# A mixture-of-experts and attention block on one core: PSUM ring banks in the true order of products, the router's products moved beside the projections, three groups of routed rows, another order of the last batch

## The reference, cut to what matters

```python
x = L0_attn_x
xn = _layernorm(x, axis=-1)
x = x + _L0_attn_ref(xn, ...) + _L0_ffn_ref(xn, ...)
# in _L0_ffn_ref:
scores = jnp.einsum("bqhd,bkhd->bhqk", q, k) * scale
probs = jax.nn.softmax(scores, axis=-1)
attn = jnp.einsum("bhqk,bkhd->bqhd", probs, v).reshape(B, T, D_MODEL)
x = _layer_norm(src + attn @ Wo + bo, ln1_g, ln1_b)
keys = (x @ router_w + router_b)[..., 0]
expert_idx = jnp.remainder(jnp.floor(keys).astype(jnp.int32), N_EXPERTS)
h = jax.nn.relu(x @ W1[e] + b1[e]); y = h @ W2[e] + b2[e]   # e = expert_idx
return _layer_norm(x + ff_out, ln2_g, ln2_b)
```

## Time and profile before

| | |
|---|---|
| median of 3 runs | 2028.31 us (2026.37 to 2028.73) |
| the profiled execution | 2027.01 us, span 2025.2 us, so 1.8 us lie around the span |
| plain attention with its end, routing | span start to 723 us |
| experts | 723 to 968 us |
| rotary attention | 968 us to the end |
| busy over the span: PE, DVE, POOL, ACT | 1809.4, 1314.8, 983.4, 829.1 us |

### The profile page before, as it was taken

How to read it: one execution, slowest core, us unless ns; L and a number is a source line. 1 busy time by engine, 2 the same in 40 slices (tenths; PEclk the granted TensorE clock), 3 DMA queues, 4 the chain that set the end, 5 groups by cost and what they waited for, 6 DMA issues and landing times.

```text
span 2025.2 us, 32126 instructions
## 1 busy us (share of the span) xinstructions
PE 1809.4 (89%) x11509; PEld 1068.3 (53%) x11510; DVE 1314.8 (65%) x2912; ACT 829.1 (41%) x1140; POOL 983.4 (49%) x631
## 2 busy tenths in 40 slices
PE   5989989889888469999489999999999999999998
PEld 2333333334333269999344655646556465564754
DVE  5767787677776537777665765657656576565760
ACT  2545545546454234444134153341533415344142
POOL 1224343452552524444437467374673746737464
PEclk7889989889898779999679999999999999999999
DMA  7427437445372455564300100101001010010000
GB/s 117 63 86 163 61 106 146 88 127 94 118 172 84 155 199 209 211 216 152 103 11 2 32 12 1 42 2 35 8 1 43 1 42 2 1 43 1 25 9 11
DMA packets 81440, 151.52 MB, mean 75 GB/s; under 512 B 11638, under 2 KB 55318, under 8 KB 75420
## 3 DMA queue, kind: packets, MB, share of 16 engines
q1 hardware_dynamic: 77980, 141.12, 26.4%
q0 software_dynamic: 3072, 8.39, 1.2%
q10 hardware_dynamic: 256, 0.26, 0.1%
HBM read 84.47 MB, written 39.85 MB: 61 GB/s over the span
## 4 chain that ended last, share of the span: by engine, by line
PE 42%; POOL 4%; DVE 3%; issue 2%; ACT 1%; DMA 0%; POOLq 0%; DVEq 0%; SPq 0%
PE a_psO L723 11%; PE a_psS L709 11%; PE a_psO L746 6%; PE a_psM L683 5%; PE a_psS L671 4%; PE a_psS L736 3%; PE a_psS L655 2%; POOL a_k_tok L356 2%; POOL a_q_tok L356 1%; ACT a_probs L474 1%; DVE a_junk L540 1%; POOL a_oT L379 1%; POOL a_probs L391 0%; DVE a_probs L510 0%; DVE a_alibi L617 0%
## 5 line engine op out<-in xcount | busy, mean ns | idle before, releaser
L391 POOL TENSOR_TENSOR a_probs<-a_probs 128x1024 f32<-128x1024 f32 x144 | 342.0, 2401 | 299.7 <-PE a_psO L723 299.7
L540 DVE CUSTOM_DVE_ANT_0 a_junk<-a_psM,a_alibi 128x512 bf16<-128x512 f32 x512 | 333.3, 688 | 198.2 <-PE a_psM L683 198.2
L1321 DVE TENSOR_REDUCE f_n_tok<-f_psR 128x1 f32<-128x512 f32 x512 | 326.4, 682 | 139.9 <-PE f_psR L1505 138.9
L474 ACT ACTIVATE a_probs<-a_psS 128x1024 f32<-128x1024 f32 x256 | 249.0, 1024 | 271.0 <-PE a_psS L709 270.1
L1265 ACT ACTIVATE f_probs<-f_psS 128x1024 f32<-128x1024 f32 x256 | 248.0, 1023 | 219.0 <-PE f_psS L1524 215.4
L1505 PE MATMUL f_psR<-f_kP,f_qP 48*128 48x512 f32 x512 | 179.9, 543 | 74.7 <-DVE f_n_tok L1321 56.4
L723 PE MATMUL a_psO<-a_probs,a_v 128*32 128x512 f32 x2048 | 244.0, 597 | 0.0
L1505 PEld LDWEIGHTS f_psR<-f_kP,f_qP 48*128 48x128 f32 x512 | 68.6, 201 | 270.1 <-DVE f_n_tok L1321 129.1
L1537 PE MATMUL f_psO<-f_probs,f_v 128*32 128x512 f32 x1024 | 148.9, 656 | 0.6 <-ACT f_probs L1265 0.6
L683 PE MATMUL a_psM<-a_kH,a_qH 64*128 64x512 f32 x512 | 122.5, 474 | 28.9 <-DVE a_n_tok L540 28.8
L746 PE MATMUL a_psO<-a_wo,a_oT 128*128 128x256 f32 x512 | 128.4, 398 | 4.4 <-POOL a_oT L379 4.4
(11 more groups left out here) (208 smaller groups left out, 3552.5 us busy)
## 6 DMA issues: line engine op xcount, KB each, us to landing
w_w_high<-w_parts SPq DMA_DIRECT2D x23, 1024.0 KB, 5.5
w_w_low<-w_parts SPq DMA_DIRECT2D x23, 1024.0 KB, 7.4
sorted_rows<-f_zeros SPq DMA_DIRECT2D x6, 1408.0 KB, 7.7
f_kP<-f_high SPq DMA_DIRECT2D x64, 128.0 KB, 5.4
f_qP<-f_high SPq DMA_DIRECT2D x64, 128.0 KB, 6.8
f_w_raw<-in_L_ffn_W SPq DMA_DIRECT2D x16, 512.0 KB, 8.1
w_parts<-f_w_high SPq DMA_DIRECT2D x16, 512.0 KB, 6.6
w_parts<-f_w_low SPq DMA_DIRECT2D x16, 512.0 KB, 8.0
```

The lines of the kernel that those rows point to most:

```text
L391: nc.gpsimd.tensor_tensor(slots, slots, probs[:, first - GRP:first - GRP + 2, :], ALU.add).then_inc(added.sem, 1)
L474: nc.scalar.activation(probs[:, slots, :], psS[:, 2 * p:2 * p + 2, :], ACT.Exp).then_inc(exp_done.sem, 1)
L540: nc.vector.tensor_tensor_reduce(out=junk[:, a, :], in0=psM[:, a, :], in1=alibi[:, h, :], scale=1.0, scalar=-3.0e38, op0=ALU.add, op1=ALU.max,
L1321: nc.vector.tensor_reduce(n_tok[:, c, column:column + 1], psR[:, ring_bank("max", u), :], AX.X, ALU.max, negate=True).then_inc(max_done.se ...
```

## The change

1. **The ring** is one list over all batches, with only the products that exist, in the order in which they are issued. The bank of each is its place in that list modulo 3, and `bank_read` waits for the reader of the product three places before.
2. **Router's products:** `weigh_rows(b-2)` goes from period (3,2) to (1,2), where the projections are, for b = 2 to 6.
3. **Statistics of norm1:** each row tile's L94 work stands directly behind the addition of that tile (`row_statistics`, periods (2,0), (2,1), (2,3), (3,0)); in (3,1) only the aggregation and the addition of epsilon are left (`aggregate_rows`).
4. **Weight chunks:** batches with three are 0 and 6 in place of 3 and 5.
5. **Last batch:** a table of its own, LAST_EXTRAS. The output projection of batch 6 goes from (2,0), (2,1), (2,3), (3,0) to (1,0) to (1,3); statistics, `finish_rows(6)`, `weigh_rows(6)` and the experts of batch 6 follow in (1,3), (2,1), (2,2), their counts in (2,3). GpSimd sends 8 tiles, then 8, and the last 8 of group 0 with the 4 of batch 6 behind its last `normalize`.
6. **Three groups:** batches 0 to 5, batch 6, batch 7. The routing phase treats 4 tiles and not 8.
7. **Landing of the scattered rows:** SP waits for it in the experts phase, behind the loads of gain and offset, and no longer GpSimd in front of the barrier.

```diff
@@ -97,6 +97,12 @@
+
+    def aggregate_rows(self, dve, b):
+        self.aggregate(dve, b)
+        dve.wait_ge(self.aggr_done.sem, self.aggr_done.at(b, self.count - 1))
...
@@ -841,14 +847,16 @@
...
-              (0, 3): [("counts", 0)],
               (3, 3): [("v", 0)]}
+    LAST_EXTRAS = {(0, 1): [("v", 1)], (0, 2): [("maxima", 1)], (0, 3): [("counts", 0)], (1, 0): [("out", 0)],
+                   (1, 1): [("out", 1)], (1, 2): [("maxima", 2), ("out", 2)], (1, 3): [("out", 3)],
+                   (2, 2): [("maxima", 3)], (2, 3): [("counts", 1)]}
...
-    MORE_CHUNKS = (3, 5)
+    MORE_CHUNKS = (0, B - 2)
@@ -862,19 +870,24 @@
...
-        if kind == "counts":
-            return b == B - 1
         return 0 <= b + belongs(kind, n) < B
 
-    ring = []
-    for r in range(PERIODS):
-        for part in maxima(r):
-            ring += [("max", u) for u in part]
-        ring += EXTRAS.get(divmod(r, TT), [])
-    ring += [None] * (-len(ring) % RING)
-
-    def ring_bank(kind, n):
-        return ring.index((kind, n)) % RING
+    def extras(b, r):
+
+        items = (EXTRAS if b + 1 < B else LAST_EXTRAS).get(divmod(r, TT), ())
+        return [(kind, n) for kind, n in items if present(b, kind, n)]
+
+    ring = [("proj", 0, n) for n in range(SIDES)] + [("v", 0, 0)] + [("max", 0, u) for u in range(AHEAD - 4)]
+    ring += [("maxima", 0, 0)] + [("max", 0, u) for u in range(AHEAD - 4, AHEAD)]
+    for b in range(B):
+        for r in range(PERIODS):
+            items = [("max", u) for part in maxima(r) for u in part if present(b, "max", u)] + extras(b, r)
+            ring += [(kind, b + belongs(kind, n), n) for kind, n in items]
+    banks = {item: i for i, item in enumerate(ring)}
...
+    def ring_bank(kind, b, n):
+
+        return banks[kind, b, n] % RING
@@ -1162,10 +1175,9 @@
...
-            def scatter_rows(first, last):
-                if first == 0:
-                    pool.wait_ge(cleared, 16 * (B - 1))
-                    pool.wait_ge(route.placed, 1)
+            def scatter_rows(group, first, last):
+                pool.wait_ge(cleared, 16 * (B - 1))
+                pool.wait_ge(route.placed, group + 1)
                 for c in range(first, last):
                     route.scatter(c, x1, sorted_x)
 
@@ -1186,30 +1198,31 @@
...
-                if not more:
-                    scatter_rows(0, 8)
+                else:
+                    scatter_rows(0, 0, 8)
+                    norm1.raise_variance(pool, b - 1)
+                    add_bias_to_rows(b)
                 normalize(b, 1)
-                add_bias_to_rows(b, not before)
                 if more:
+                    add_bias_to_rows(b, not before)
                     keep_rows(b + 1)
+                    for n in chunks_of(b)[:1]:
+                        split_chunk(n)
+                    if before:
+                        scale_rows(b - 1)
                 else:
-                    scatter_rows(8, 16)
-                for n in chunks_of(b)[:1]:
-                    split_chunk(n)
-                if not more:
-                    norm1.raise_variance(pool, b - 1)
-                elif before:
-                    scale_rows(b - 1)
+                    scatter_rows(0, 8, 16)
                 normalize(b, 2)
-                if not more:
-                    scatter_rows(16, EARLY * TT)
-                elif before:
-                    finish_rows(b - 1)
-                for n in chunks_of(b)[1:]:
-                    split_chunk(n)
+                if more:
+                    if before:
+                        finish_rows(b - 1)
+                    for n in chunks_of(b)[1:]:
+                        split_chunk(n)
...
+            scatter_rows(0, 16, EARLY * TT)
+            scatter_rows(1, EARLY * TT, (EARLY + 1) * TT)
             norm1.raise_variance(pool, B - 1)
 
@@ -1379,31 +1392,38 @@
...
-                    if (quad, j) == (3, 2) and 2 <= b < B - 1:
-                        weigh_rows(b - 2)
-                    if (quad, j) == (0, 0) and not more:
-                        weigh_rows(b - 2)
-                    if (quad, j) == (0, 1) and not more:
-                        route.find_experts(dve, 0)
-                    if (quad, j) == (0, 0) and more:
-                        dve.wait_ge(x_in.sem, x_in.at(b + 1, 0))
-                        norm0.statistics(dve, b + 1, xn)
-                    if (quad, j) == (0, 2) and more:
-                        norm0.apply(dve, b + 1, xn, xn, xn_done)
-                    if (quad, j) == (3, 1) and before:
-                        dve.wait_ge(r1_done.sem, r1_done.at(b - 1, TT - 1))
-                        norm1.statistics(dve, b - 1, r1)
-                    if (quad, j) == (3, 3) and not more:
-                        finish_rows(b - 1)
+                    for kind, n in extras(b, r):
+                        if kind == "out":
+                            add_rows(b - 1, n, psR[:, ring_bank(kind, b - 1, n), :])
+                            dve.wait_ge(r1_done.sem, r1_done.at(b - 1, n))
+                            norm1.row_statistics(r1, n)
+                        elif kind == "v":
+                            add_bias(b, n)
+                        elif kind == "counts":
+                            route.take_sums(dve, n, psR[:, ring_bank(kind, b, n), :])
+                            route.find_places(dve, n)
+                    if more:
+                        if (quad, j) == (0, 0):
+                            dve.wait_ge(x_in.sem, x_in.at(b + 1, 0))
+                            norm0.statistics(dve, b + 1, xn)
+                        elif (quad, j) == (0, 2):
+                            norm0.apply(dve, b + 1, xn, xn, xn_done)
+                        elif (quad, j) == (1, 2) and b >= 2:
+                            weigh_rows(b - 2)
+                        elif (quad, j) == (3, 1) and before:
+                            norm1.aggregate_rows(dve, b - 1)
+                    else:
+                        if (quad, j) == (0, 0):
+                            weigh_rows(b - 2)
+                        elif (quad, j) == (0, 2):
+                            route.find_experts(dve, 0)
+                        elif (quad, j) == (1, 3):
+                            norm1.aggregate_rows(dve, b - 1)
+                        elif (quad, j) == (2, 1):
+                            finish_rows(b - 1)
+                        elif (quad, j) == (2, 2):
+                            weigh_rows(b - 1)
+                            route.find_experts(dve, 1)
 
@@ -1421,7 +1441,6 @@
...
-            weigh_rows(B - 2)
@@ -1434,27 +1453,20 @@
             pv_done.grant(pe)
             pe.wait_ge(weights_in, WEIGHTS)
 
-            def bank_read(b, kind, n):
-
-                i = ring.index((kind, n)) - RING
-                while i > -len(ring):
-                    item, cycle = ring[i], b - 1 if i < 0 else b
-                    if item is not None and present(cycle, *item) and (cycle, item) != (-1, ("v", 0)):
-                        signal, k = read[item[0]](item[1])
-                        pe.wait_ge(signal.sem, signal.at(cycle + belongs(*item), k))
-                        return
-                    i -= RING
-
-            def project(b, kind, n, first=False):
+            def bank_read(kind, b, n):
+
+                i = banks[kind, b, n] - RING
+                if i >= 0:
+                    signal, k = read[ring[i][0]](ring[i][2])
+                    pe.wait_ge(signal.sem, signal.at(ring[i][1], k))
+
+            def project(b, kind, n):
 
                 batch = b + belongs(kind, n)
                 if n == 0 and kind == "proj":
                     pe.wait_ge(xnT_sb.sem, xnT_sb.at(batch, KC - 1))
-                if first:
-                    pe.wait_ge(high_done.sem, high_done.at(0, SIDES - 1))
-                else:
-                    bank_read(b, kind, n)
-                bank = psR[:, ring_bank(kind, n), :]
+                bank_read(kind, batch, n)
+                bank = psR[:, ring_bank(kind, batch, n), :]
                 if kind == "v":
                     for k in range(2):
                         t = 2 * n + k
@@ -1600,7 +1610,7 @@
...
-    GROUPS = ((0, (B - 2) * TT), ((B - 2) * TT, B * TT))
+    GROUPS = ((0, (B - 2) * TT), ((B - 2) * TT, (B - 1) * TT), ((B - 1) * TT, B * TT))
@@ -1842,23 +1851,22 @@
...
-            pool.wait_ge(route.placed, 2)
-            for c in range(*route.GROUPS[1]):
+            pool.wait_ge(route.placed, 3)
+            for c in range(*route.GROUPS[2]):
                 route.scatter(c, x1, sorted_x)
-            pool.wait_ge(route.scattered, 16 * CT)
 
         @block.tensor
         def _(pe):
             pe.wait_ge(weights.o1_in, 16)
             rows = NE * FF // P
             nc.tensor.transpose(psB[:, 0:rows], weights.o1_rows[:, :], weights.idn[0:rows, 0:rows]).then_inc(o1_ps, 1)
-            route.count_rows(pe, 1, psR)
+            route.count_rows(pe, 2, psR)
 
         @block.vector
         def _(dve):
```

(6 more changed lines are left out.)

57 lines of the change are left out of this document (24 added, 33 removed).

## The result

The changed kernel takes 2009.54 us (median of 7 runs, 2003.92 to 2013.81), the kernel before on the same chips 2026.37 (7 runs, 2017.94 to 2029.30): ratio 0.9917, 95% interval 0.9902 to 0.9932, so 17 us and not the 48.7 of the forecast. It is faster, and outside the range of 1960 to 1997. The profiled execution took 2005.31 us, 21.7 us under that of before and 4.2 us under the median of its own kernel; the ledger is that of this one pair.

| Stretch | forecast, us | measured, us |
|---|---|---|
| quad 0 of batches 4 and 6 (chunks) | -12.6 | -14.4 |
| quad 3 of batches 0 to 6, with the seam | -20.4 | -17.8 |
| quads 1 and 2 of batches 0 to 6 | 0 to +0.5 each batch | +6.7 in all |
| quad 0 of batches 1, 2, 3, 5; start | 0 | +0.4 |
| batch 7 up to its last psO copy | -1 | +9.4 |

What follows compares the result with a forecast made beforehand. The prediction took what precedes the experts' first rows, plain attention and routing, as all the change can move. Terms -12.6, -17.5, -2.9, -1, -8.0, -5.1 and -1.6 sum to -48.7 us, 2027.0 to 1978.3, stated as 1979 us; range 1960 to 1997.

Steps and rivals of the forecast that it cites:

- Chunks, -12.6: Quad 0 of batches 4 and 6: moving the third weight chunks away gives 6.3 us for each of two batches.
- Seams, -20.4: Seams between batches: 3.5 us at each of five, -17.5 us, and -2.9 us together at the two outer ones.
- (a): Ring at each of 7 seams: TensorE no longer waits 0.84 us for the reader of "v" 0.
- (b): Statistics leave (3,1): L106 asked for 0.9 us earlier, a tie with GpSimd's L1143; if first, VectorE is free 2.2 us earlier.
- (d): Addition of epsilon in (0,0): asked for before L1143, so VectorE is free at 522.9, not 525.15; 2.2 us a seam.
- rival 5: Seams and end: seam gains are waited for in the next quads, landings bound the end; 2026 us, chance 0.02.
- The -2.9 for the two outer seams: Seams 0/1 and 6/7: the ring alone, and the ring plus the first router's product (2.53 us against 0.41), -2.9 us together.
- Row statistics, 0 to 0.5 each batch: Periods (2,0) to (3,0): moved statistics fall into VectorE gaps of 0.4 to 1.2 us, costing 0 to 0.5 us.
- Last batch, -1: Batch 7: a new 3.5 us wait at the counts against output projections moved into quad 1; -1 us, bounds -4 and +5.
- Rival 3: Last batch: TensorE pauses in (1,0) for `normalize`, or over 5 us at the counts; chance 0.12.
- End, -8.0: Last `weigh` to root of batch 7: 12.5 us instead of 20.5, as scatters no longer stand in front; -8.0 us.
- Routing, -5.1 and -1.6: Between places and experts: four scatters fewer, -5.1 us; barrier and two loads beside the landing, -1.6 us.

Runs made afterwards that it cites:

- the six profiles: Profiles of the changed kernel twice and of four experiments that touch only what comes after batches 1 to 6; those batches take 446.1 to 468.3 us.

## Why the prediction was wrong

The change wins 17 us and not 48.7 because the sum counted waits that were taken out as time won, without asking what TensorE and VectorE would wait for next. The largest misses of the profiled pair are the last batch (10.4 us), quads 1 and 2 (6.7), the end (4.9) and the first rows (4.0); at the seams the number came out near the forecast, the steps to it did not.

- *Chunks, -12.6:* right. The two quads gave 14.4 us (7.9 to 14.4 in the six profiles), and undoing it costs 10.7. The cover in batch 6 held, but by luck: the `normalize` behind the third chunk ends 20.0 us into quad 0 of batch 7 and not 15.5. The 18.3 us at which I had the output projection would have been too early; it came at 28.2, since TensorE had paused 7.00 us for VectorE.
- *Seams, -20.4:* two steps held, one failed and one bound was missing, so that the -17.8 is near the forecast by luck (-8.5 to -20.4 in the six profiles). (a) The ring alone gives 8.6 us. (b) The tie went to VectorE at all six seams, and putting the statistics back loses it at all six. (d) Failed: the addition in (0,0) runs into the cast L1154, or behind it into L1156, and took 0.2 to 2.3 us, 6.5 us in all after 7.8 before. I had read its 1.75 us at one seam and taken it for all. It lies behind the copy of psO, so its gain would stand in quad 0, not in the row of the seams; the quads 0 of batches 1, 2, 3 and 5 are 1 us longer in all. I had called it won because it would be asked for during the cast, and had not asked whether the cast stops VectorE too. The failed step is from a won addition to TensorE's time (0.84 + 2.2 + 1.3 us a seam with (a) and (b) won): a quad 3 got 2.0 us shorter on average (129.0 to 117 for six), because behind the stall stood the landing of the maxima in f_qP, 8.2 us from transposes to scores, which no term named. To move the maxima ahead is worth 17.7 us on the changed kernel and 3 to 7 on the ring alone. My rival 5 had it in words ("waited for in the next quads") with a chance of 0.02. The -2.9 for the two outer seams was also added up wrong: two rings and the product are 0.84 + 0.84 + 2.1 = 3.8 us.
- *Products in (1,2), 0:* right, as far as the intervals tell; moving them back changes nothing that is seen.
- *Row statistics, 0 to 0.5 each batch:* quads 1 and 2 lost 1 us a batch, but with the statistics away quad 2 stays within 0.3 us. It is the landing in f_qP again, which no term named: TensorE waits 0.7 to 0.8 us for it in quad 1, where it hardly waited before, and 0.4 to 1.0 in quad 2 (0.4 to 0.5). With the maxima moved ahead the loss is gone. Why the landing bounds these quads now is open.
- *Last batch, -1, the largest miss:* it became 9.4 us longer. The counts' wait of 3.5 us was 4.8, quads 2 and 3 gave only 4.2 us beside it and not 6, and quad 1 grew by 3.1 and not 2. The failed step is the seam of 6 and 7: I took a gain from the first of the router's products and did not ask when GpSimd has their rows ready. Quad 3 ahead of it became 5.7 us shorter (22.4 to 16.7), GpSimd's work did not, and it finishes the rows of batch 5 at 584.62, 3.9 us after VectorE asks: 7.00 us of TensorE. Moving the products to (0,2) gives quad 0 its 6.7 us back, of which 1.4 come back in quad 1. Rival 3 had its sign and place, with other causes.
- *End, -8.0:* the cover of the scatters held (they end 4.77 us ahead of the root). The failed step is "2.4 us for additions and statistics": beside the scatters the last of VectorE's additions ends 7.2 us behind the last projection, where it was 0.5 us in the kernel before; without them the last `weigh` to the last addition is 7.6 us.
- *Routing, -5.1 and -1.6:* the four scatters gave 5.0. The failed step is the 1.6: the barrier stayed 6.6 us behind the last scatter with the wait or without, and the rows, issued earlier against the weights' loads (10 us and not 15 behind the first of them), took 2.4 us longer.

By the table the misses are +2.6 at the seams, +6.7 in quads 1 and 2, +0.4, +10.4 in the last batch, +4.9 at the end, +4.0 in routing and -1.8 at the chunks: 27 us, from 1978.3 to 2005.3.

## What to carry to other kernels

Where a stall is taken out, list for the waiting engine every other input of its next instruction with the time at which it arrives, transfers too: the second latest is the new bound, and here it could be had for one constant and a table: 18 to 20 us once it was the bound, 3 to 7 before. Add up the waiting engine's idle time over the whole stretch, before and after: here it fell by 3 us where single waits fell by far more. When an engine is moved ahead, its producers have to be moved ahead as well, most of all in the batch that is ordered otherwise. Small gains in different places added up here only after each was read in its own stretch.

## What the runs showed of the hardware

- Beside GpSimd's indirect scatters, issued back to back, VectorE's additions of a PSUM and an SBUF operand started 3 to 7 us late, in steps of some 0.7 us, while beside 425 GB/s of plain loads they did not. In the kernel before and with the ring alone the same additions ran beside such scatters without a gap (1.72 us for four). What differs, and by what way the scatters act, is not shown.
- GpSimd's cast L1154 stops VectorE as L1156 does: 0.92 us for an addition of 0.17 that ended with it, and 1.02 us for L1701, 0.18 elsewhere.
- The end of the routing block comes 6.3 to 6.8 us behind the end of GpSimd's last scatter, whether the program waits for the transfers or not. The block of plain attention ended 3.2 us behind it in the three kernels where its scatters came last; what makes the difference is not shown.
- SyncE's 128 KB moves of f_high to f_qP, not the small ones of the maxima, land 7.3 to 8.1 us after their issue (median) in the fifteen kernels made from the changed one, and 6.7 to 6.8 in the three with the batches' order of before. Why is open.
